# Attention and expert block on one core: another order for a batch's output merge, and another place for masks and expert weights

## What is computed

```python
def _L0_attn_ref(x, Wq, Wk, Wv, Wo):
    q = split_heads(x @ Wq)
    k = split_heads(x @ Wk)
    v = split_heads(x @ Wv)
    qc = q - q.mean(axis=-1, keepdims=True)
    kc = k - k.mean(axis=-1, keepdims=True)
    cov = jnp.einsum('bhsd,bhtd->bhst', qc, kc) / D
    ...
    scores = cov + var_comp
    attn = jax.nn.softmax(scores, axis=-1)
    out = jnp.einsum('bhst,bhtd->bhsd', attn, v)
    ...
    return out @ Wo
...
xn = _layernorm(x, axis=-1)
x = x + _L0_attn_ref(xn, ...) + _L0_ffn_ref(xn, ...)
```

## Time and profile before

| | |
|---|---|
| median of three runs | 1299.82 us |
| lowest and highest | 1298.62, 1304.07 us |
| the profiled execution | 1300.59 us, of which the trace spans 1298.3 |
| busy in the span | PE 1127.0 (87%), DVE 989.6 (76%), ACT 796.9 (61%), POOL 375.9 (29%) |
| attention stage | steps from about 13 to 620 us |

### The profile page before, as it was taken

One profiled execution on the slowest core, in us unless ns is written; L12 is line 12 of the kernel. 1 busy time (PEld: TensorE's weight loads), 2 busy tenths in 40 slices (PEclk: granted clock), 3 DMA queues, 4 the chain that ended last, 5 costly groups with the idle time before them and its releaser, 6 DMA issues.

```text
span 1298.3 us, 33300 instructions
## 1 busy us (share of the span) xinstructions
PE 1127.0 (87%) x11462; PEld 669.0 (52%) x11462; DVE 989.6 (76%) x2827; ACT 796.9 (61%) x1440; POOL 375.9 (29%) x644
## 2 busy tenths in 40 slices
PE   1498888888888888888769999999999999999998
PEld 0234444444444444443236666666666666666676
DVE  2767887888888888876467888787888887897773
ACT  0046665666666666666647666777667677667744
POOL 5343554444445555540021011111011110011000
PEclk9999997999999999997778999999999999999999
DMA  3000000000000000000010110000000000000000
GB/s 95 5 10 15 15 17 17 17 17 17 13 17 13 17 17 17 17 11 27 5 46 1 26 26 6 20 24 24 24 19 5 24 24 24 24 11 14 18 10 17
DMA packets 50452, 24.90 MB, mean 19 GB/s; under 512 B 5984, under 2 KB 49888, under 8 KB 50400
## 3 DMA queue, kind: packets, MB, share of 16 engines
q1 hardware_dynamic: 50400, 24.21, 6.9%
HBM read 15.28 MB, written 8.39 MB: 18 GB/s over the span
## 4 chain that ended last, share of the span: by engine, by line
PE 43%; POOL 19%; ACT 17%; issue 11%; DVE 8%; ACTq 1%; POOLq 0%; DMA 0%; SPq 0%; DVEq 0%
PE bank L558 39%; ACT Kexp L1383 7%; ACT hmid L1458 4%; POOL xn L431 4%; POOL stack L461 3%; ACT prob L1361 3%; POOL sq L443 2%; DVE smax L1053 2%; PE bank L599 2%; POOL rstd L428 2%; POOL sq L445 2%; POOL stack L456 2%; ACT prob L1394 1%; POOL feat L453 1%; DVE prob L1057 1%
## 5 line engine op out<-in xcount | busy, mean ns | idle before, releaser
L975 DVE TENSOR_REDUCE rowmin<-bank 128x2 f32<-128x512 f32 x512 | 336.9, 687 | 119.0 <-PE bank L558 114.7
L1361 ACT ACTIVATE prob<-bank 128x512 f32<-128x512 f32 x512 | 301.4, 607 | 204.8 <-PE bank L558 203.8
L558 PEld LDWEIGHTS bank<-w_sb,hmid 128*128 128x128 f32 x2048 | 244.0, 192 | 24.1 <-issue 12.3
L558 PE MATMUL bank<-w_sb,hmid 128*128 128x128 f32 x2048 | 248.5, 276 | 0.2 <-issue 0.2
L1458 ACT ACTIVATE hmid<-bank,up_scale 128x512 f32<-128x512 f32 x256 | 175.9, 732 | 111.3 <-PE bank L558 111.1
L558 PE MATMUL bank<-QKT 32*128 32x256 f16 x2048 | 199.4, 285 | 31.9 <-ACT prob L1361 15.4
L1383 ACT ACTIVATE Kexp<-bank,head_bias,head_mask 128x512 f32<-128x512 f32 x256 | 187.8, 846 | 42.5 <-PE bank L558 42.5
L1266 DVE SCALAR_TENSOR_TENSOR acc<-bank,gate,acc 128x128 f32<-128x128 f32 x512 | 143.3, 342 | 72.9 <-PE bank L558 70.8
L487 POOL TENSOR_TENSOR rstd<-mv,epsilon 128x4 f32<-128x4 f32 x16 | 8.9, 553 | 503.9 <-DVE mv L1204 503.9
L558 PEld LDWEIGHTS bank<-QKT 32*128 32x128 f16 x2048 | 68.0, 94 | 155.6 <-issue 68.4
L558 PE MATMUL bank<-prob,V 128*25 128x256 f32 x2048 | 147.3, 408 | 0.0
(11 more groups left out here) (177 smaller groups left out, 1622.4 us busy)
## 6 DMA issues: line engine op xcount, KB each, us to landing
x_in<-in_L_attn_x SPq DMA_DIRECT2D x32, 128.0 KB, 2.1
z_scratch<-z_out SPq DMA_DIRECT2D x32, 128.0 KB, 1.8
xg<-in_L_attn_x SPq DMA_DIRECT2D x64, 64.0 KB, 2.0
zg<-z_scratch SPq DMA_DIRECT2D x64, 64.0 KB, 1.9
out<-acc SPq DMA_DIRECT2D x64, 64.0 KB, 1.6
QKT<-shiftT SPq DMA_DIRECT2D x128, 4.0 KB
w_sb<-in_L_ffn_w SPq DMA_DIRECT2D x1, 1024.0 KB, 6.1
wo<-in_L_attn_Wo SPq DMA_DIRECT2D x16, 4.0 KB
```

The costliest lines, as they stand in the source:

```text
L558: return pe.matmul(o, l, r, start=start, stop=stop, skip_group_check=True)
L975: dve.tensor_reduce(rowmin[h // 8][:, :, h % TILE_ROWS, h // TILE_ROWS % HALF], row_scores[i % 3][:].rearrange("p (s t) -> p s t", s=ST), ...
L1361: act.activation(prob[:, h % 8].rearrange("p t s -> p (t s)"), col_scores[h % 2][:], ACT.Exp, scale=exp_register).then_inc(s_exp, 1)
```

## The change

Two things are moved, with nothing else in the calculation changed but where w1's bound is multiplied in.

1. In a step, PE's half0 transposes go from place 8 to 7, the merge transposes from 5 to 9 (six places behind "out", just ahead of the xn transposes), and the output projection from 11 to 12. DVE's copy of half0 goes from 9 to 8 and its statistics from 0 to 2; ACT's copy oT_all goes from 6 to 10, just ahead of xnT. As half0 now uses bank 6 before the merge, the waits change: half0 waits for `s_on` (o_nat is made), and the merge for `s_half[0]` (DVE has copied half0).
2. `masks` stands before step 1 of POOL's stream, `prepare` before step -2 of DVE's (behind `zero`) and of PE's. `head_bias`, which needs the masks, is made by DVE before step 2. w1 isn't multiplied by its bound any more; the bound goes into the maximum and the scale instead.

```diff
-PE_AT = dict(half1=0, out=3, merge=5, half0=8, project=11, v=2, shift0=6, x=9, qk=11, shift1=14)
-DVE_AT = dict(half1=1, statistics=0, out=4, shift0=5, half0=9, shift1=12)
-ACT_AT = dict(copy_out=2, v=3, merged=6, shift0=7, x=10, features=12, output=13, shift1=15)
+PE_AT = dict(half1=0, out=3, half0=7, merge=9, project=12, v=2, shift0=6, x=9, qk=11, shift1=14)
+DVE_AT = dict(half1=1, statistics=2, out=4, shift0=5, half0=8, shift1=12)
+ACT_AT = dict(copy_out=2, v=3, merged=10, shift0=7, x=10, features=12, output=13, shift1=15)
...
-            run_steps(pool, step, {-2: masks})
+            run_steps(pool, step, {1: masks})
...
-                    if h == PE_AT["merge"] and prev:
-                        merge_transposes(b - 1)
                     if h == PE_AT["half0"] and prep:
                         if prev:
-                            pe.wait_ge(s_oa, b)
+                            pe.wait_ge(s_on, b)
                         elif nxt:
                             pe.wait_ge(s_half[1], b + 2)
                         stack_transposes(b + 2, 0)
-                    if h == PE_AT["project"] and prev:
+                    if h == PE_AT["merge"] and prev:
                         if prep:
                             pe.wait_ge(s_half[0], b + 3)
+                        merge_transposes(b - 1)
+                    if h == PE_AT["project"] and prev:
                         project_out(b - 1)
...
-            run_steps(pe, step, {-1: prepare})
+            run_steps(pe, step, {-2: prepare})
...
             def prepare():
 
-                dve.wait_ge(s_ident, 3)
-                dve.wait_ge(s_vones, QUAD)
                 dve.wait_ge(s_dma_w2, 16 * 11)
...
-                dve.tensor_scalar(head_bias[:], head_mask[:], in_bT[:, 1:2], None, ALU.mult)
-
...
                 dve.reciprocal(hn2_scale[:], bound[:]).then_inc(s_dve, 1)
-                dve.tensor_scalar(w1_sb[:], w1_sb[:], bound[:, 0:1], None, ALU.mult).then_inc(s_dve, 1)
-                own.next()
...
-                dve.tensor_tensor(w1_max[:], w1_max[:], w1_scale[:], ALU.max).then_inc(s_setup, 1)
+                dve.tensor_tensor(w1_max[:], w1_max[:], w1_scale[:], ALU.max).then_inc(s_dve, 1)
+                dve.wait_ge(s_dve, own.next())
+                dve.tensor_tensor(w1_max[:], w1_max[:], bound[:], ALU.mult).then_inc(s_setup, 1)
...
-                dve.tensor_scalar(w1_scale[:], w1_scale[:], W1_TOP, None, ALU.mult).then_inc(s_dve, 1)
+                dve.tensor_scalar(w1_scale[:], w1_scale[:], bound[:, 0:1], W1_TOP, ALU.mult, ALU.mult).then_inc(s_dve, 1)
...
-            run_steps(dve, step, {-2: zero, -1: prepare})
+            def start():
+                zero()
+                prepare()
+
+            def biases():
+                dve.wait_ge(s_ident, 3)
+                dve.wait_ge(s_vones, QUAD)
+                dve.tensor_scalar(head_bias[:], head_mask[:], in_bT[:, 1:2], None, ALU.mult).then_inc(s_setup, 1)
+
+            run_steps(dve, step, {-2: start, 2: biases})
```

More of the change, by code:

```diff
@@ L683, in hn_transposes @@
                     pe.wait_ge(s_max, H * NB)
-                    pe.wait_ge(s_setup, 4)
+                    pe.wait_ge(s_setup, 5)
                 if positive(n):
@@ L1421, in first_head @@
                 if slot == ACT_FIRST["hn"]:
-                    act.wait_ge(s_setup, 4)
+                    act.wait_ge(s_setup, 5)
                     hn_out(0)
```

## The result

| | before | after |
|---|---|---|
| median on the same chip | 1299.22 us (4 runs, 1296.66 to 1304.07) | 1399.05 us (4 runs, 1393.06 to 1404.0) |
| ratio, 95% interval | | 1.0762 (1.0706 to 1.0817) |
| profiled execution, span | 1300.59, 1298.3 | 1393.06, 1391.1 |
| mean granted clock of TensorE | 0.972 | 0.904 |

The change makes the kernel 7.6% slower. The forecast was 2.5% slower, 1332 us; its range ended at 1350. Direction and ring were right, and a cost of some 60 us was missed.

The account below looks back on a forecast made before the run. The prediction took a ring of waits through POOL's sq-to-xn work, 17.03 us a step, to bound the kernel. 1.35 us over 27 steps gave 1300.6 + 36.5 + 0.6 - 5.0 = 1332.7, forecast 1332 us, range 1307 to 1350.

Parts of the forecast that it names:

- ring: Chain of waits repeated each attention step, from half1 through POOL's sq to xn, projection and exp: 17.03 us, growing by 1.35.
- forecast 0.75: Merge waiting for DVE's copy of half0 delays the xn transposes: +0.75 us a step, bounds 0 and 1.0.
- forecast 1.1: Sign in the profile after: the merge (L661) waits about 1.1 us for DVE's QKT copy.
- over 1: Sign in the profile after: PE's wait at shift0 is over 1 us.
- The copy of oT_all: On ACT at place 10, ahead of xnT, it delays what follows: +0.25 us a step, low bound 0.
- The output projection: Behind place 12 it no longer runs while PE waits for xnT: +0.35 us a step, bounds 0.1 to 0.57.
- 1.35: Sum of the ring's terms for merge, oT_all copy and output projection, in us a step: a step of 18.4 us.
- the forecast's own case: Whole kernel slower, at 1322 to 1341 us; chance 0.56.
- The first rival: Ring stays bound by POOL, merge hidden in the wait for xn: faster, 1290 us, chance 0.05; 1258 form, 0.03.
- 1258: Form of the faster rival: removing PE's 1.32 us wait shortens 28 steps by 37 us in all; chance 0.03.
- the last rival: Clock falls more often: one to four more stretches at 1.2 GHz, 1338 to 1352 us; chance 0.13 for over 1341.
- The start: Weights and masks prepared in the first steps: xn transposes of batch 4 at 99.4 not 104.51, -5.0 us, bounds -6.5 and -1.

Follow-up runs that it names:

- part 5: Three runs of the kernel before with score products repeated at places 5 and 10, at 5 only, at 10 only: ratios 1.0163, 0.9896, 1.0337.
- {10: 2}: Kernel before with the pair of score products at place 10 computed two more times, gap before the merge left open: 1345.02 us, ratio 1.0337.
- part 7: Here the kernel after with the old tables and PE order, so the new start alone against the kernel before: 1298.79 us, ratio 1.0002.
- {10: 5}: Kernel before with the pair of score products at place 10 computed five more times: 1353.51 to 1375.75 us, ratio 1.0457.
- the filled runs: Score products repeated in TensorE's gaps: kernel after with all three gaps filled, 1337.86 us; kernel before with place 5 filled, 1290.23 us.
- e4: Kernel after, gaps not filled, with the merge transposes at place 10 and ACT's oT_all at 11: 1398.82 us, ratio 1.0758.
- {5: 5}: Kernel before with the pair of score products at place 5, ahead of the merge, computed five more times: 1290.23 us, ratio 0.9896.

## Why the prediction was wrong, point by point

- **The ring was read rightly.** From POOL's sq to the xn transposes are 410.35 - 400.46 = 9.89 us, against 9.19 before: +0.70 for the forecast 0.75. The merge waits 1.14 us for DVE's copy (forecast 1.1), shift0 1.50 (over 1). The copy of oT_all costs some 0.3 (0.25); xnT starts 0.25 behind it. The output projection costs some 0.3 (0.35). The sum is 1.3 for 1.35; the full-clock step was 18.40 to 18.48 for the forecast 18.4. Some 0.1 us of the step's growth from 17.03 has no owner in the runs. Without the clock's loss, the kernel is at 1337.9, inside the forecast's own case of 1322 to 1341.
- **The first rival fell.** POOL doesn't set the step any more, and its xn is waited for in no steady step. The Trainium skill (Perfetto Trace Analysis, Identifying Performance Opportunities) sends one to the gaps of the most-contended engine. If the step had shrunk by that gap, the time would have been 1258; the wait for o_nat did go, and the time rose by 100. But the same gap filled with work, instead of emptied by moving, gave 1% (part 5), with the full-clock step still 17.03: what it cost was the clock, not the wait.
- **The step that failed** is the clock, for which the sum 1300.6 + 36.5 + 0.6 - 5.0 has no term. It stands only in the last rival, "The clock falls more often", with the right direction and the wrong size: "one to four more such stretches" and a chance of 0.13. It happened in every step of the profiled run. 61 us against the rival's 6 to 20 is nearly the whole of the miss: 1332 + 61 = 1393, against the 1399 measured; 4 of the other 6 us are the start's gain that did not arrive (below). The error in reasoning was the sentence "in this trace the other slices of steady steps, with their gaps of 1.3 us, read 9". It took one gap in one step length for proof that gaps of this size are harmless. `{10: 2}` shows the same gap in a step longer by 0.44 us losing the clock in ten of 27 steps. And the trace of before held a sign that was overlooked. The one fall that slice 7 shows begins in this very gap:

```profile
202.62 0.69 PE L661 MATMUL bank<-ident,o_nat 128*128 128x128 f32 x2 [1.32 <-DVE o_nat L999]
203.24 1.92 PE L558 MATMUL bank<-prob,V 128*25 128x256 f32 x16
```

  The merge takes 0.69 us instead of 0.44, the pv products 1.92 instead of 1.06; the granted clock is 1.00 up to 201.9 and 0.51 from there to 215.7. In `{10: 2}` each of the ten falls begins 0.5 to 0.9 us behind the end of the same gap.
- **The start** moved as worked out up to its xn: sq of batch 3 at 82.11 (forecast 83.9), xn transposes of batch 4 at 97.78 (99.4). But of the forecast -5.0 only -1.0 reached sq of batch 4. The rows of after:

```profile
82.11 1.04 POOL L443 TENSOR_TENSOR sq<-feat 128x512 f32<-128x512 f32 x1 [10.68 <-PE bank L599]
...
97.78 0.66 PE L574 MATMUL bank<-ident,xn 128*128 128x128 f32 x2 [4.88 <-POOL xn L431]
...
111.21 1.04 POOL L443 TENSOR_TENSOR sq<-feat 128x512 f32<-128x512 f32 x1 [13.57 <-PE bank L599]
```

  The wait of 4.88 us behind the masks was in the forecast as a delay. That TensorE would run at 1.2 GHz from 89.4 to 113.2 us was not. The clock fell ahead of that wait, just behind the new gap of 1.50 us before shift0 (88.84). With the old steps (part 7), 4.9 us of the gain reach sq of batch 4.

**What stays open** is why the same gaps bring the clock down in one step and not in the next. It follows a pattern: none of the steps of 17.03 us but one, every second or third at 17.47, mostly every fourth at 18.4 with gaps of 0.5 to 0.6, all with 1.50 and 1.14. Filling adds work and removes idle time at once, so that a threshold on the one or the other isn't shown either; but `{10: 5}` and `{10: 2}` only added work, and fell.

## What to carry to other kernels

When an edit changes the length of a step, or opens gaps of around a microsecond in TensorE's stream, count the clock as a term of the sum, not as a rare accident: here it cost more than the ring did. That the gaps of today's steps are harmless is no proof for a step of another length. Where the clock does fall in a trace, look what stood just before: here it was the gap. A cheap test is to fill the gap with work that computes again what is already there, no longer than the gap. If the kernel gets faster, the gap costs clock; the next thing to do is to put useful work there.

## What the runs showed of the hardware that was not expected

- TensorE's granted clock fell to 1.2 GHz once in every steady step of after, where TensorE was busy 458 of 566 us and no gap was over 1.6 us. Filling the gaps brought it back in both kernels: 0.84 to 0.99 in the steady steps of after, with 0.3 us as the longest gap left. The Trainium skill (TensorE: Matmul & The Clock Gate, What's actually happening) says that the throttled clock is the default and that activity releases it. By that, more work in the gaps should keep the clock up, and the filled runs agree.
- A microsecond at 1.2 GHz cost much less than half of itself here: 2.4 us more per fallen step of `{10: 2}`, in which TensorE was at 1.2 GHz for 6.8 (68.3 us in ten stretches). In e4's kernel 84 us went for 266 at 1.2 GHz. The rest was hidden in waits that were there anyway. But as the falls recur each step, it adds up.
- Early in a trace the page's clock row can read 9 while TensorE is slow: before, it reads 9 in the first slices, but eight half1 transposes take 1.03 us at 51.06 and 0.62 in a steady step. The duration of a known product is the surer sign.
- Useless work made a tuned kernel 1% faster. The mean granted clock of the four runs of `{5: 5}` is 0.979 to 0.983, that of the runs of before beside them 0.960 to 0.972.
